# Attention layer: a third probability tile transposed by the side path, the cosine product on VectorE out of PSUM, and a new order of work on all engines

## The reference

```python
h = _layernorm(x) * (1 + ca) + sa
q = apply_rotary(pos, proj(Wq, bq) * DIM_HEAD ** -0.5)   # 16 heads of 128
k = apply_rotary(pos, proj(Wk, bk))                      # t * cos + rotate_half(t) * sin
sim = where(causal, -max, einsum('bhid,bhjd->bhij', q, k))
out = einsum('bhij,bhjd->bhid', softmax(sim), proj(Wv, bv))
x = x + ga * (out.reshape(b, n, 2048) @ Wo + bo)
x = x + gb * ffn(_layernorm(x) * (1 + cb) + sb)          # gated, 704 wide
```

## Time and profile before

| what | value |
|---|---|
| median of 3 runs | 1033.11 us (1029.83 to 1033.45) |
| profiled execution | 1031.39 us, span 1029.6 us |
| granted TensorE clock | 0.996 of full speed |
| busy PE, PEld | 970.8 us (94%), 854.3 us (83%) |
| busy DVE | 784.1 us (76%) |
| busy POOL | 764.7 us (74%) |
| busy ACT | 669.5 us (65%) |
| chain that ended last | PE 62%, POOL 11%, issue 7%, DMA 7%, ACT 6%, DVE 4% |
| DMA | 116.74 MB, mean 113 GB/s |

### The profile page before, as it was taken

One profiled execution on the slowest core, in us unless ns is written; L12 is line 12 of the kernel. 1 busy time (PEld: TensorE's weight loads), 2 busy tenths in 40 slices (PEclk: granted clock), 3 DMA queues, 4 the chain that ended last, 5 costly groups with the idle time before them and its releaser, 6 DMA issues.

```text
span 1029.6 us, 19698 instructions
## 1 busy us (share of the span) xinstructions
PE 970.8 (94%) x5853; PEld 854.3 (83%) x5853; DVE 784.1 (76%) x1605; ACT 669.5 (65%) x1385; POOL 764.7 (74%) x532
## 2 busy tenths in 40 slices
PE   6988999999999999999999999999999999998897
PEld 5877888888888888888888888888888788887787
DVE  6857877777788788877787778877887777877644
ACT  5756656676666666666666666666666567767763
POOL 3487877788778877787778878787778777885653
PEclk9999999999999999999999999999999999999999
DMA  7524443343334433443434333543344335431011
GB/s 248 166 79 139 118 118 101 107 131 114 102 101 139 127 113 111 138 127 100 115 97 141 103 111 97 148 127 107 107 142 124 109 99 159 139 103 42 1 42 42
DMA packets 86597, 116.74 MB, mean 113 GB/s; under 512 B 10468, under 2 KB 61732, under 8 KB 86564
## 3 DMA queue, kind: packets, MB, share of 16 engines
q1 hardware_dynamic: 86564, 116.33, 39.2%
HBM read 50.17 MB, written 32.57 MB: 80 GB/s over the span
## 4 chain that ended last, share of the span: by engine, by line
PE 62%; POOL 11%; issue 7%; DMA 7%; ACT 6%; DVE 4%; SPq 2%; ACTq 0%; POOLq 0%; DVEq 0%
PE ps_r L1504 13%; PE ps_r L1503 13%; PE ps_r L1502 13%; PE ps_s L1502 5%; PE ps_s L1504 4%; PE ps_s L1503 4%; PE ps_t L1663 4%; POOL swapped L734 3%; DMA swapped<-straight 3%; POOL qk_lo L744 3%; POOL straight L735 2%; DMA side_out<-squares 2%; DMA side_p<-side_out 2%; ACT straight L885 2%; ACT probs L1014 1%
## 5 line engine op out<-in xcount | busy, mean ns | idle before, releaser
L734 POOL TENSOR_TENSOR swapped<-swapped,sin_sb 128x512 f32<-128x512 f32 x124 | 167.5, 1351 | 135.5 <-DMA swapped<-straight 135.0
L1014 ACT ACTIVATE probs<-ps_s,neg_max 128x128 f32<-128x128 f32 (+7 forms) x256 | 190.2, 743 | 109.3 <-DVE neg_max L1394 109.3
L1394 DVE CUSTOM_DVE_ANT_0 ps_s<-ps_s,mask_wide 128x128 f32<-128x128 f32 (+7 forms) x256 | 193.4, 755 | 31.1 <-PE ps_s L1504 29.4
L744 POOL TENSOR_TENSOR qk_lo<-straight,qk_hi 128x512 fp32r<-128x512 f32 x124 | 161.8, 1315 | 63.3 <-ACT qk_hi L898 63.2
L1314 DVE TENSOR_TENSOR pT_lo<-ps_t,pT_hi 128x512 fp32r<-128x512 f32 (+3 forms) x260 | 126.7, 498 | 75.7 <-ACT pT_hi L992 75.6
L735 POOL TENSOR_TENSOR straight<-straight,cos_sb 128x512 f32<-128x512 f32 x124 | 181.8, 1466 | 0.0
L1235 DVE TENSOR_TENSOR straight<-straight,swapped 128x512 f32<-128x512 f32 x126 | 147.1, 1168 | 15.2 <-POOL straight L735 14.7
L754 POOL TENSOR_TENSOR pT_lo<-side_p,pT_hi 128x1024 fp32r<-128x1024 f32 (+1 forms) x62 | 150.9, 2434 | 0.0
L1502 PE MATMUL ps_s<-qk_hi 128*128 128x512 f32 (+4 forms) x384 | 139.8, 364 | 9.7 <-POOL qk_lo L744 9.5
L992 ACT ACTIVATE pT_hi<-ps_t 128x512 fp32r<-128x512 f32 (+3 forms) x260 | 117.1, 450 | 43.0 <-PE ps_t L1663 41.3
L1353 DVE SCALAR_TENSOR_TENSOR y<-ps_r,inv_sum,y 128x256 f32<-128x256 f32 x248 | 108.4, 479 | 35.7 <-PE ps_r L1504 31.7
(11 more groups left out here) (201 smaller groups left out, 2391.0 us busy)
## 6 DMA issues: line engine op xcount, KB each, us to landing
swapped<-straight SPq DMA_DIRECT2D x252, 128.0 KB, 2.3
side_out<-squares SPq DMA_DIRECT2D x31, 512.0 KB, 2.6
side_p<-side_out SPq DMA_DIRECT2D x124, 128.0 KB, 3.0
side_out<-squares SPq DMA_DIRECT2D x31, 448.0 KB, 2.5
side_p<-side_out SPq DMA_DIRECT2D x124, 112.0 KB, 2.5
x_in<-in_L_attn_x SPq DMA_DIRECT2D x4, 512.0 KB, 5.5
w_raw<-in_L_attn_Wk SPq DMA_DIRECT2D x8, 256.0 KB, 3.2
w_raw<-in_L_attn_Wq SPq DMA_DIRECT2D x8, 256.0 KB, 3.8
```

What stands on the lines that cost most here:

```text
L734: pool.tensor_tensor(swapped[:, q, :], swapped[:, q, :], sin_sb[:, cs], ALU.mult)
L744: pool.tensor_tensor(lo, rope_buffers(piece)[0][:, RANK[piece] % 2, :], hi.bitcast(F32), ALU.subtract)\
L1014: nc.scalar.activation(halved(t, probs[:, P_AT[step] * P:(P_AT[step] + t + 1) * P]), score_rows(step, t), ACT.Exp, bias=neg_max[:, t:t + 1 ...
L1394: nc.vector.tensor_tensor_reduce(rows, rows, halved(t, mask_wide[:, SEQ - n_keys:SEQ]), -1.0, -MASKED, ALU.add, ALU.min, accum_out=neg_max ...
```

## The change

**The 768-key tile goes aside.** `SIDE` is now 7, 6 and 5. In units 0 to 30 the tokens `turn:5.0` and `turn:5.1` drop out on TensorE, ScalarE and VectorE (six transposes, two copies, two subtractions a unit), and `side:5`, `back:5` come in. Each side tile has a buffer `side_p` of its own.

**The cosine product on VectorE.** VectorE reads the projection out of PSUM, adds the bias and multiplies by the cosine in one instruction, into `qk_cos` (which lies where `qk_lo` does). GpSimd multiplies `swapped` by the sine as before, waits for that and for `cos_ready`, and adds `qk_cos` to it. So GpSimd still has three operations for each piece (product, sum, low part) and VectorE has the one product where it had the sum. A bank of a q or k piece is now free when VectorE is through with it, and not after ScalarE's copy.

**Squares.** `squares` may be overwritten when the DMA that writes it out has landed; before, VectorE waited until the tile had been read back. `move_back` now waits for the low part of the unit before.

**The scale of q** is folded into the weights (`w_high` for ScalarE, `wq_low`, which is VectorE's now and was GpSimd's `w_low`).

**Order.** All five plans of a unit are written anew; unit 31 takes its P1 where it did.

```diff
-SIDE = (7, 6)
+SIDE = (7, 6, 5)
...
-TENSOR_PLAN = """make:K0+ make:Q0+ scores:0 turn:6.0- turn:7.0- scores:1 scores:2 turn:7.1- make:P0- turn:0.0
+TENSOR_PLAN = """scores:0 turn:6.0- make:K0+ make:Q0+ turn:7.0- scores:1 make:P0- scores:2 turn:7.1- make:K1+ make:Q1+
...
-SYNC_PLAN = """swap:K0+ swap:Q0+ side:1 back:1 swap:K1+ swap:Q1+ side:3 back:3"""
+SYNC_PLAN = """swap:K0+ swap:Q0+ side:1 back:1 side:3 swap:K1+ swap:Q1+ back:3 side:5 back:5"""
...
+        elif what == "turn" and v >= 0 and has_side(v, int(name[0])):
+            continue
...
                 sp.wait_ge(straight_ready, ps.rank(piece, 1))
+                if RANK[piece] >= 6:
+                    sp.nop(nofuse=True)
+                    sp.wait_ge(qk_ready, ps.rank(piece, -1))
...
+                for v, other in ((u, 7), ) if t == 4 else ((u - 1, 4 if t == 7 and 4 in SIDE else t), ):
+                    if v >= 0:
+                        sp.wait_ge(side_ready[other], ps.units_done(v))
+                        sp.nop(nofuse=True)
                 sp.wait_ge(side_written[t], ps.units_done(u, 16))
...
-                pool.tensor_tensor(swapped[:, q, :], swapped[:, q, :], sin_sb[:, cs], ALU.mult)
-                pool.tensor_tensor(straight[:, q, :], straight[:, q, :], cos_sb[:, cs], ALU.mult).then_inc(rotated, 1)
+                pool.tensor_tensor(swapped[:, q, :], swapped[:, q, :], sin_sb[:, at_], ALU.mult).then_inc(rotated, 1)
+                pool.wait_ge(cos_ready, ps.cosines(piece))
+                pool.wait_ge(rotated, ps.rank(piece, 1))
+                pool.tensor_tensor(swapped[:, q, :], swapped[:, q, :], qk_cos[:, unit % 2, which, at_], ALU.add).then_inc(qk_sum, 1)
...
-                if RANK[piece] >= 4:
+                if RANK[piece] >= 6:
+                    act.wait_ge(swapped_ready[q], ps.swaps(piece, 2))
+                elif RANK[piece] >= 4:
                     act.wait_ge(qk_ready, ps.rank(piece, -1))
...
+            def wq_low(n):
+                raw, hi, lo = w_buffers[WQ]
+                dve.wait_ge(w_hi_ready[WQ], n + 1)
+                nc.vector.scalar_tensor_tensor(lo, raw, SCALE, hi.bitcast(F32), ALU.mult, ALU.subtract).then_inc(w_ready[WQ], 1)
...
+            def qk_cosine(ps, piece):
...
+                dve.wait_ge(straight_ready, ps.rank(piece, 1))
...
+                nc.vector.scalar_tensor_tensor(qk_cos[:, unit % 2, which, at_], ps_r[:, ps.bank(piece), :], bias, cos_sb[:, at_],
+                                               ALU.add, ALU.mult).then_inc(cos_ready, 1)
...
-                    dve.wait_ge(side_landed[ORDER[before]], ps.units_done(v, 16 * SIDE_DMAS))
+                    dve.wait_ge(side_written[ORDER[before]], ps.units_done(v, 16))
...
-                    pe.wait_ge(straight_ready, ps.rank(old, 1))
+                    if old in FIRST_QK:
+                        pe.wait_ge(straight_ready, ps.rank(old, 1))
+                    else:
+                        pe.wait_ge(cos_ready, ps.cosines(old))
```

More of the change, by code:

```diff
@@ L124 @@
     SCALAR_PLAN: """exp:0 out:K0+ xout:4 xout:5 exp:1 out:Q0+ xout:6 xout:7 exp:2 turn:0.0 exp:3 high:K0+ high:Q0+
-        side:1 exp:4 out:K1+ turn:2.0 out:Q1+ exp:5 turn:4.0 high:V0 high:V1 high:K1+ turn:5.0 exp:6 split:O side:3 turn:5.1 high:Q1+""",
-    VECTOR_PLAN: """max:0 max:1 xlow:4 xlow:5 max:2 side:1 max:3 add:K0+ xlow:6 xlow:7 turn:0.0 sum:B0 add:Q0+ sum:B1
-        max:4 gates:0 turn:2.0 side:3 max:5
-        turn:4.0 max:6 low:V0 add:K1+ low:V1 max:7 turn:5.0 add:Q1+ turn:5.1""",
@@ L129 @@
[L129 to L142 removed]
+        exp:4 out:K1+ turn:2.0 out:Q1+ side:1 exp:5 turn:4.0 high:V0 high:V1 high:K1+ turn:5.0 exp:6 split:O side:3 turn:5.1 high:Q1+""",
@@ new lines @@
+    VECTOR_PLAN: """max:0 cos:K0+ max:1 xlow:4 cos:Q0+ xlow:5 max:2 side:1 max:3 xlow:6 xlow:7 turn:0.0 sum:B0 sum:B1
+        max:4 gates:0 cos:K1+ turn:2.0 side:3 max:5 cos:Q1+
+        turn:4.0 side:5 max:6 low:V0 low:V1 max:7 turn:5.0 turn:5.1""",
+    POOL_PLAN: """rotate:K0+ rotate:Q0+ low:K0+ low:Q0+ rotate:K1+ rotate:Q1+ low:K1+ low:Q1+ side:1 side:3 bias:0 split:O"""}
+PLANS_30 = {
+    TENSOR_PLAN: """scores:0 turn:6.0- make:K0+ make:Q0+ turn:7.0- scores:1 make:P0- scores:2 turn:7.1- make:K1+ make:Q1+
+        turn:0.0 scores:3 make:W00- scores:4 make:P1- turn:2.0 scores:5 make:W01- make:W10- turn:4.0 scores:6
+        make:W11- make:L0 make:L1 scores:7 make:L2 make:L3 make:L4 make:L5""",
+    SCALAR_PLAN: """exp:7- out:K0+ turn:6.0- out:Q0+ turn:7.0- exp:0 float:3 side:5- high:P0- exp:1 turn:7.1- out:K1+ exp:2
+        out:Q1+ high:K0+ turn:0.0 exp:3 high:Q0+ high:P1- exp:4 turn:2.0 exp:5 side:1 exp:6 high:K1+ side:3
+        high:Q1+ turn:4.0 out:L0 out:L1 out:L2 out:L3 out:L4 out:L5""",
+    VECTOR_PLAN: """cos:K0+ turn:6.0- max:0 turn:7.0- cos:Q0+ max:1 largest:0 max:2 low:P0- side:1 turn:7.1- cos:K1+ cos:Q1+
+        max:3 side:3 sum:W00- max:4 turn:0.0 low:P1- max:5 largest:1 sum:W01- sum:W10- max:6 sum:W11- side:5
+        turn:2.0 max:7 largest:2 turn:4.0"""}
@@ L270, in groups, with swaps, cosines @@
         return self.count(u * T_UNIT + first_group(u, step) + more, UNITS * T_UNIT)
+    def swaps(self, piece, earlier=0):
+        return self.count((RANK[piece] - 4 - earlier) // 2 * 32 + 32, PER_PASS["qk"] // 2 * 32)
+    def cosines(self, piece):
+        return self.count(RANK[piece] - 3, PER_PASS["qk"])
     def sides(self, u, step, more=0):
@@ L459, in build @@
         pT_ready = sem("pT_ready")
+        cos_ready = sem("cos_ready")
         squares_ready = sem("squares_ready")
@@ L654, in run @@
                     n = u // UNITS + 1
-                    for what, _, piece in unit_plan(SYNC_PLAN, u):
+                    for what, x, piece in unit_plan(SYNC_PLAN, u):
                         if what == "swap":
@@ L884, in qk_out @@
                 bias = (bq_s if which == 0 else cols[:, COL_BK:COL_BK + HEADS])[:, bass.ds(head, 1)]
-                nc.scalar.activation(rope_buffers(piece)[0][:, q, :], ps_r[:, ps.bank(piece), :], ACT.Identity, bias=bias,
-                                     scale=SCALE if which == 0 else 1.0).then_inc(straight_ready, 1)
+                nc.scalar.activation(rope_buffers(piece)[0][:, q, :], ps_r[:, ps.bank(piece), :], ACT.Identity, bias=bias)\
+                    .then_inc(straight_ready, 1)
             def gate_out(ps, piece):
@@ L1454, in do @@
                     gate_columns()
+                elif what == "split":
+                    wq_low(ps.passes(piece))
                 else:
-                    {"qk": qk_add, "v": v_low, "pv": o_low, "wo": wo_add, "bias": bias_row}[piece[0]](ps, piece)
+                    {"qk": qk_cosine, "v": v_low, "pv": o_low, "wo": wo_add, "bias": bias_row}[piece[0]](ps, piece)
             def run(ps):
```

94 lines of the change are left out of this document (43 added, 51 removed).

## The result

The changed kernel takes **990.0 us** (median of 4 runs, 988.37 to 992.03), the kernel before 1032.4 us beside it (4 runs, 1029.83 to 1033.45): ratio 0.959, 95% interval 0.957 to 0.962. The forecast was 995 us in a range of 968 to 1020. The profiled execution took 992.03 us, its span is 990.1 us.

What follows compares the result with a forecast made beforehand. TensorE's own work was taken to bound the loop: 28.0 - 0.65 (transposes) - 0.64 (waits) = 26.7 us a unit. Then 1031.4 - 39 - 0.7 + 3 = 994.7, given as 995 us, range 968 to 1020.

Steps and rivals of the forecast that it cites:

- The forecast case: Whole kernel: 26.4 to 27.0 us a unit, 986 to 1004 us, chance 0.52.
- the signs named beforehand: Trace: passes 106 to 108 us, VectorE busy near 82, GpSimd 93 to 96, TensorE idle near 1 us a pass.
- Transposes, 0.65 us a unit: TensorE: six transposes of the 768-key tile go, 0.108 us each, in 31 units, 20 us in all.
- The waits, 0.64 of 0.89 us: TensorE in the loop: of 0.89 us idle a unit, 0.25 stays and 0.64 goes.
- third case: TensorE: all 0.89 us goes, 984 us; with half the weight loads' waits, 25.9 a unit, 967 us; chance 0.15.
- Unit 31 and the end, +3: Unit 31: P1 as early as before, 768-key tile last on GpSimd; costs nothing to 8 us, 3 taken.
- 20.6 us a unit and 750 ns: VectorE: busy time falls from 22.2 to 20.6 us a unit; each cosine product out of PSUM takes 750 ns.
- (b): TensorE's Q0, needing V1 out of its bank: 0.8 us early if VectorE is not behind; 0.2 to 0.4 wait likely.
- 24.0 us a unit at most: GpSimd: busy time rises from 22.1 to at most 24.0 us a unit with the third tile's low part.
- The contention that I left out of the sum: GpSimd: losing VectorE's sum of two SBUF tiles beside it could give back 0.6 us, four times 0.15.
- The slow rival: GpSimd becomes the bound: 29.9 us a unit, loop 57 us longer, 1088 us; chance 0.10.
- threshold of 4.0 us idle a unit: GpSimd: its becoming the bound decides from 4.0 us of idle time a unit on (28.0 - 24.0).

Runs made afterwards that it cites:

- experiment 7: Changed kernel with six of TensorE's transposes in each unit made twice: 1002.93 us, ratio 0.971 against the kernel before.
- experiment 2: Changed kernel with only tiles 7 and 6 aside, the 768-key tile turned on TensorE again, turns taken early on VectorE and ScalarE: 1006.75 us.
- experiment 9: Changed kernel with unit 29's six integer-weight loads moved behind the swaps of K0 and Q0: 983.54 us alone, 976.97 us with the loop written out.
- experiment 5: Changed kernel with VectorE doing the cosine product of each piece twice: 1046.69 us, ratio 1.015 against the kernel before.
- experiment 6: Changed kernel with GpSimd making the 768-key side tile's low part twice: 994.71 us, ratio 0.965 against the kernel before.
- experiment 4: Changed kernel with the squares taken until the tile is back from memory, as in the kernel before: 1058.27 us, ratio 1.025.
- experiment 3: Changed kernel's instructions put in the order of the kernel before: 1082.29 us with two tiles aside, 1197.87 us with three.

## Why the prediction came out right

The forecast case held (986 to 1004), but its terms were off, and they made up for each other. For the 24 units between the side copies of units 4 and 28 the forecast is 24 x 1.3 = 31.2 us, and 41.2 were measured; for what lies behind it is about even, and 9.0 were lost. That the sum came within 5 us is in part luck. Of the signs named beforehand two missed: a pass is 105.3 us and not 106 to 108, and GpSimd is busy 90.0 us of it and not 93 to 96.

- **Transposes, 0.65 us a unit.** Right: experiment 7 gives 0.70. The third tile gives 0.88 us a unit in the loop (21.1 us over 24 units, experiment 2), since it ends waits too; over the whole kernel it is worth 16.8 us, 20 in the prediction.
- **The waits, 0.64 of 0.89 us.** TensorE's idle time fell as said, to 0.31 us a unit (0.25 in the prediction). But a pass got 6.7 us shorter and not 5.2. The step that failed is taking TensorE's idle time for all its waiting. The starts of its matmuls tell more. I take the distance from each start to the next, less the usual spacing (0.231 us for 512 columns, 0.175, 0.147, 0.119 and 0.110 for the shorter ones), and add these up over a pass: 5.7 us before, 1.6 now, and -0.1 in the written-out loop, where TensorE has no idle time. Of the 5.7 only 3.57 were idle time; the rest lay under the recorded length of the matmul before. One such place in the trace before: at 435.49 us the weight load had waited 0.62 us and the matmul 0.19, and 0.35 us more than usual lay between the two starts. So a part of the weight load's 2.9 and 1.6 us in the earlier trace rows belonged in the sum. The 4.1 and 24 x 0.108 for the transposes make the 6.7. The prediction had this as its third case, at 0.15 (its 984 and 967 us leave out the +3 for the end that the forecast has).
- **No jump.** Without it the unit would be 25.9 us, which is the end of that third case. The jump's 1.7 us a pass stood in no term, and covers a part of what the waits gave beyond the forecast. The trace of before could not show it, as its round loads no code.
- **Unit 31 and the end, +3.** Right for what it was meant for: from unit 30's first side copy on the kernel got 3.5 us longer (126.2 to 129.7). The two units ahead of it, 28 to 30 by their side copies, were to get 2.6 shorter and got 5.5 longer (56.4 to 61.9). The loads ahead of the swaps are 6.9 us of it (61.9 to 55.0 in experiment 9), a term that the prediction put at nothing. The order in SyncE's queue was in the diff's reach, and I didn't go through it there: the third tile's way back now stands ahead of the loads, and the loads ahead of K0's swap.
- **VectorE.** 20.6 us a unit and 750 ns were right (82.1 a pass, 744). That it had room was not: experiment 5 puts the price of one more microsecond in the product at 0.6. The prediction's (b), "here it is even", fits better.
- **GpSimd.** 24.0 us a unit at most, measured 22.5, with 3.8 idle. The contention that I left out of the sum gave most of these 1.5 us back (0.6 estimated): by the means of the operations, 0.7 for the four sums, 0.35 for the 1024-key low part and 0.2 for the sine products. The Trainium skill, SBUF — State Buffer, Who interferes with whom, gave the direction, and the trace agrees, with 1466 to 1299 and 2745 to 2397 ns. The slow rival, GpSimd as bound, is refuted by experiment 6. Its threshold of 4.0 us idle a unit was worked out with 24.0 of work (28.0 - 24.0); with 22.5 it is 5.5, and 3.8 were measured. Against the unit's own length an idle time says little, since a shorter unit leaves less of it.
- **The squares free once written.** It had no term at all, and experiment 4 shows that the sign of the whole change hangs on it: 68 us. With three tiles through one staging area the way back (2.3 to 2.9 us from issue to landing) no longer fits between them in this order.

The parts don't add: in the old order, as placed there, the product loses 49 us, and with the third tile 165 (experiment 3); in the new one the two gain 42.
